# Attention outputs split into 16-bit halves and turned by a crossbar DMA transpose

## What is computed

```python
x = x + 0.5 * _L0_ffn_ref(_layernorm(x, axis=-1), ...)     # ternary weights, 128 -> 512 -> 128
x = x + _L0_attn_ref(_layernorm(x, axis=-1), ...)          # 16 heads of 64, causal, gated outputs
x = x + 0.5 * _L0_ffn_ref(_layernorm(x, axis=-1), ...)
x = x + 0.5 * _L1_ffn_ref(_layernorm(x, axis=-1), ...)     # 8 experts, the best 2 of each token
x = x + _L1_attn_ref(_layernorm(x, axis=-1), ...)          # 16 heads of 64, causal
x = x + 0.5 * _L1_ffn_ref(_layernorm(x, axis=-1), ...)
```

## Time and profile before

| | |
|---|---|
| time, median of 3 runs | 1004.79 us |
| the 3 runs | 1001.63, 1004.79, 1005.98 us |
| span of the profiled execution, first to last instruction | 1000.9 us |
| busy: TensorE / VectorE / GpSimd / ScalarE | 90% / 79% / 73% / 67% of the span |
| TensorE's granted clock, mean | 0.978 of full speed |
| first attention: first to last `project_out` | 72.2 to 362.1 us |
| second attention: the same | 561.6 to 838.2 us |

### The profile page before, as it was taken

One profiled execution on the slowest core, in us unless ns is written; L12 is line 12 of the kernel. 1 busy time (PEld: TensorE's weight loads), 2 busy tenths in 40 slices (PEclk: granted clock), 3 DMA queues, 4 the chain that ended last, 5 costly groups with the idle time before them and its releaser, 6 DMA issues.

```text
span 1000.9 us, 33897 instructions
## 1 busy us (share of the span) xinstructions
PE 897.1 (90%) x13160; PEld 640.5 (64%) x13160; DVE 792.1 (79%) x2394; ACT 673.5 (67%) x1183; POOL 734.7 (73%) x685
## 2 busy tenths in 40 slices
PE   5789999999999879899987899999999985998884
PEld 3467676776777656566654676777677764666663
DVE  6889898888889877777656889888888887866563
ACT  6688888878877626556555787767767762545552
POOL 6789989889887745666545999878888883666662
PEclk9999999999999979999999999999999997999997
DMA  5201011010030001122111000000000001121222
GB/s 153 78 10 45 3 45 45 3 45 2 3 107 3 2 20 39 52 43 85 38 30 51 3 3 3 12 3 2 13 3 3 13 2 30 41 43 44 86 62 82
DMA packets 21118, 33.79 MB, mean 34 GB/s; under 512 B 4578, under 2 KB 10466, under 8 KB 20964
## 3 DMA queue, kind: packets, MB, share of 16 engines
q1 hardware_dynamic: 13728, 18.50, 5.9%
q0 software_dynamic: 5888, 12.07, 4.8%
q10 hardware_dynamic: 1348, 1.05, 0.3%
HBM read 22.44 MB, written 9.18 MB: 32 GB/s over the span
## 4 chain that ended last, share of the span: by engine, by line
PE 63%; DVE 18%; ACT 6%; issue 6%; POOL 3%; another core or an unknown queue 2%; DMA 1%; SPq 0%; POOLq 0%; DVEq 0%; ACTq 0%
PE ps L1698 8%; PE ps L1889 8%; PE ps L1700 8%; PE ps L1699 7%; DVE arena L1308 4%; PE ps L1919 3%; PE ps L2128 3%; PE ps L1853 3%; PE ps L1920 3%; PE ps L1921 3%; PE ps L2140 2%; PE ps L2141 2%; PE ps L2142 2%; PE ps L1864 2%
## 5 line engine op out<-in xcount | busy, mean ns | idle before, releaser
L784 POOL TENSOR_TENSOR arena<-arena 128x1024 f16<-128x1024 f32 x190 | 344.9, 1816 | 86.2 <-ACT arena L980 75.9
L1308 DVE CUSTOM_DVE_ANT_0 arena<-ps,mask_qk 128x512 bf16<-128x512 f32 (+3 forms) x512 | 224.4, 485 | 25.0 <-PE ps L1853 23.8
L972 ACT ACTIVATE arena<-ps,lift 128x1024 f32<-128x1024 f32 (+1 forms) x192 | 186.7, 972 | 85.0 <-PE ps L1899 82.2
L1889 PE MATMUL ps<-arena 64*128 64x512 f16 (+3 forms) x1536 | 148.5, 299 | 10.2 <-ACT arena L972 6.8
L835 POOL DMA_INDIRECT arena<-x_rows,arena x92 | 92.6, 1006 | 88.5 <-PE ps L2103 43.7
L1919 PE MATMUL ps<-arena 128*128 128x65 f16 x1280 | 130.9, 195 | 0.2 <-DVE arena L1332 0.2
L1920 PE MATMUL ps<-arena 128*128 128x64 f16 x1280 | 130.4, 193 | 0.0
L1921 PE MATMUL ps<-arena 128*128 128x65 f16 x1280 | 130.0, 194 | 0.0
L843 POOL DMA_INDIRECT y_rows<-arena x92 | 90.8, 987 | 49.0 <-ACT arena L1138 26.1
L1919 PEld LDWEIGHTS ps<-arena 128*128 128x128 f16 x1280 | 117.4, 98 | 8.4 <-issue 0.5
L1920 PEld LDWEIGHTS ps<-arena 128*128 128x128 f16 x1280 | 117.9, 99 | 0.2 <-issue 0.2
(11 more groups left out here) (288 smaller groups left out, 2695.9 us busy)
## 6 DMA issues: line engine op xcount, KB each, us to landing
stage<-in_L_ffn_W SPq DMA_DIRECT2D x4, 1024.0 KB, 5.3
arena<-y_rows SPq DMA_DIRECT2D x14, 256.0 KB, 3.6
x_rows<-XN SPq DMA_DIRECT2D x8, 256.0 KB, 2.1
arena<-x_rows,arena POOLq DMA_INDIRECT x92
y_rows<-arena POOLq DMA_INDIRECT x92
stage<-in_L_attn_Wkv SPq DMA_DIRECT2D x2, 512.0 KB, 8.3
X<-in_L_attn_tokens SPq DMA_DIRECT2D x3, 256.0 KB, 5.1
out_x<-X SPq DMA_DIRECT2D x3, 256.0 KB
```

The lines of the kernel that those rows point to most:

```text
L784: g.tensor_tensor(PL[:, b, :, cols], P32[:, :, cols], PH[:, b, :, cols], ALU.subtract).then_inc(s_pl, 1)
L972: a_.activation(P32[:, :, UNIT_AT[u]:UNIT_AT[u] + UNIT_W[u]], ps[:, 4:6, 0:UNIT_W[u]], ACT.Exp, bias=lift[:]).then_inc(s_ex_p, 1)
L1308: v_.tensor_tensor_reduce(masked[:, x, 0:w], ps[:, 2 + x, at:at + w], mask_qk[:, CH - w:CH], 1.0, NEG, ALU.add, ALU.max, accum_out=MX[:, i ...
L1889: mm(ps[:, 4 + x, at:at + w], keys, queries, start=(n_ == 0 and part == 0), stop=False)
```

## The change

The outputs are no longer turned as float32 by TensorE. They are split where they stand, with tokens on partitions, and both halves are turned by one DMA through the crossbar, issued by SyncE:

1. ScalarE rounds `O32` to float16 into `OS[:, 0]` (`output_high`), at the place of `turned_high`.
2. VectorE subtracts into `OS[:, 1]` (`output_low`), at the place of `turned_low`.
3. SyncE waits for that and issues one `dma_start_transpose` of `OS` (128 partitions x 1024 float16, 256 KB) into `OT` (128 x 2 x 4 x 128), which lies in the memory of `T32`.
4. TensorE waits for the DMA before `project_out`, which reads `OT`.

TensorE's four transposes per item and their bank are gone, so `outputs(1)` no longer waits for `turned_low`. SyncE's program is rewritten so that its other DMAs stand between the transposes, at given turns. The second normalization writes its intermediate in place into PSUM, since `T32` is taken.

```diff
-        OTh = carve([CH], F16)
-        OTl = carve([CH], F16)
+        OS = carve([2, CH], F16)
+        OT = T32[:].bitcast(F16).rearrange("p (k i d) -> p k i d", k=2, i=TPB)
...
+            def attention(a):
+                base = a * ITEMS
+                def body(t):
+                    o = items(t)[4]
+                    if o is not None:
+                        j = base + o
+                        sp.wait_ge(s_o_lo, j + 1)
+                        if j >= 1:
+                            sp.wait_ge(s_op_ps, j)
+                        sp.dma_start_transpose(OT.rearrange("p k i d -> p (k i) d"), OS.rearrange("p k c -> p (k c)")
+                                               ).then_inc(s_o_turned, 16)
+                    if a == 0 and t == 0:
+                        expert_block(0)
+                    if a == 0 and t == 1:
+                        expert_block(1)
+                    if a == 0 and t in (6, 10, 14, 18):
+                        expert_block((t - 6) // 4 + 2)
+                    if a == 0 and t == 27:
+                        second_layer()
+                    if t in ROWS_OUT[a]:
+                        rows_out(*ROWS_OUT[a][t])
+                run_items(body, range(TURNS))
+            ROWS_OUT = ({20: (3, 0), 28: (3, 1)}, {13: (5, 0), 21: (5, 1), 29: (5, 2)})
...
-                    def turned_high():
+                    def output_high():
                         j = base + o
-                        act.wait_ge(s_ot_ps, j + 1)
-                        if o >= 1:
-                            act.wait_ge(s_op_ps, j)
-                        a_.activation(OTh, ps[:, 7, :], ACT.Copy).then_inc(s_oth_sb, 1)
+                        act.wait_ge(s_o_ev, j + 1)
+                        if j >= 1:
+                            act.wait_ge(s_o_turned, 16 * j)
+                        a_.activation(OS[:, 0], O32.rearrange("p a x d -> p (a x d)"), ACT.Copy).then_inc(s_o_hi, 1)
...
-                    step(v_.tensor_scalar(T32[:], src, gamma[:], beta[:], ALU.mult, ALU.add))
-                    ins_ = v_.tensor_tensor(l, T32[:], h, ALU.subtract)
+                    step(v_.tensor_scalar(src, src, gamma[:], beta[:], ALU.mult, ALU.add))
+                    ins_ = v_.tensor_tensor(l, src, h, ALU.subtract)
...
-                    def turned_low():
-                        dve.wait_ge(s_oth_sb, base + o + 1)
-                        v_.tensor_tensor(OTl, ps[:, 7, :], OTh, ALU.subtract).then_inc(s_otl_sb, 1)
+                    def output_low():
+                        dve.wait_ge(s_o_hi, base + o + 1)
+                        v_.tensor_tensor(OS[:, 1], O32.rearrange("p a x d -> p (a x d)"), OS[:, 0], ALU.subtract
+                                         ).then_inc(s_o_lo, 1)
...
-                        elif v >= 1:
-                            pe.wait_ge(s_otl_sb, j)
...
-                    def turn_outputs():
-                        pe.wait_ge(s_o_ev, base + o + 1)
-                        for i in range(TPB):
-                            ins_ = nc.tensor.transpose(ps[:, 7, i * P:(i + 1) * P],
-                                                       O32[:, i].rearrange("p x d -> p (x d)"), ident[:])
-                        ins_.then_inc(s_ot_ps, 1)
-
                     def project_out():
-                        pe.wait_ge(s_otl_sb, base + o + 1)
+                        pe.wait_ge(s_o_turned, 16 * (base + o + 1))
...
-                            blk = slice(i * P, (i + 1) * P)
-                            split_mm(ps[:, 1, i * D:(i + 1) * D], OTh[:, blk], OTl[:, blk],
+                            split_mm(ps[:, 1, i * D:(i + 1) * D], OT[:, 0, i], OT[:, 1, i],
                                      WOh[:, o % PAIRS], WOl[:, o % PAIRS], s_op_ps if i == TPB - 1 else None)
```

More of the change, by code:

```diff
@@ L342, in macaron_block @@
         s_o_ev = sem("o_ev")
-        s_ot_ps = sem("ot_ps")
-        s_oth_sb = sem("oth_sb")
-        s_otl_sb = sem("otl_sb")
+        s_o_hi = sem("o_hi")
+        s_o_lo = sem("o_lo")
+        s_o_turned = sem("o_turned")
         s_op_ps = sem("op_ps")
@@ L574, in _, with expert_block @@
             sp.dma_start(wg_in[:, HEADS:HEADS + EXPERTS], ins["L1_ffn_Wg"]).then_inc(s_wa_in[4], 16)
-            for i, (src, hi, lo) in enumerate(experts):
+            def expert_block(i):
+                src = experts[i][0]
                 if i == 0:
@@ L587, in _, with second_layer @@
                 sp.dma_start(dst, src).then_inc(s_e_in[i % 2], 16)
[L589 to L592, removed]
+            def second_layer():
+                sp.wait_ge(s_lo_pool, 2 + 4 * len(experts))
+                flat = stage[:].rearrange("p a b -> p (a b)")
+                sp.dma_start(flat[:, 0:3 * INNER].rearrange("p (c d) -> p c d", d=D), wqkv1).then_inc(s_w1_in, 16)
+                sp.dma_start(flat[:, 3 * INNER:4 * INNER], wout1).then_inc(s_w1_in, 16)
@@ new lines, in rows_out, with results_in @@
+            def rows_out(n, c):
+                sp.wait_ge(s_ln_xn, NORM_NO[n, c])
+                at = c % HCH * CH
+                sp.dma_start(x_rows[c // HCH][at:at + CH].rearrange("(p t) d -> p t d", t=TPC),
+                             XN[:, TPC * c:TPC * (c + 1), :]).then_inc(s_x_rows[c // HCH], 16)
+            def results_in(m, h):
+                for k in range(YRING):
+                    sp.wait_ge(s_y_out[k], moved(m, k, HT * (h + 1)))
+                for c in range(HCH * h, HCH * (h + 1)):
+                    for j in range(TOPK):
+                        at = j * TOK + c * CH
+                        sp.dma_start(Yt[:, c, j], y_rows[at:at + CH].rearrange("(p t) d -> p t d", t=TPC)
+                                     ).then_inc(s_y_got[c], 16)
@@ L604, in end_loads @@
                              ).then_inc(s_out_done, 16)
[L606 to L622, removed]
             x_out = out.rearrange("b (t p) d -> p (b t) d", p=P)
@@ L631, in stored @@
                                  ).then_inc(s_out_done, 16)
-            moe(3, 0)
-            moe(5, 1)
+            attention(0)
+            rows_out(3, 2)
+            rows_out(3, 3)
+            results_in(0, 0)
+            results_in(0, 1)
+            attention(1)
+            rows_out(5, 3)
+            results_in(1, 0)
+            stored(0)
             end_loads()
@@ L1033, in body @@
                     if o is not None:
-                        turned_high()
+                        output_high()
                     if s is not None:
@@ L1359, in evacuate @@
                         if v >= 1:
-                            dve.wait_ge(s_ot_ps, j)
+                            dve.wait_ge(s_o_lo, j)
                         v_.tensor_tensor(O32.rearrange("p a x c -> p x a c"), o4[:, :, :, 0:DH],
@@ L1390, in body @@
                     if o is not None:
-                        turned_low()
+                        output_low()
                     if t == TURNS - 3:
@@ L1955, in body @@
                             project_k()
-                    if o is not None:
-                        turn_outputs()
                     if s is not None:
```

## The result

| | before | after |
|---|---|---|
| median | 1005.98 us | 1075.44 us |
| runs | 1001.63 to 1009.18 us (5) | 1072.96 to 1082.27 us (5) |
| profiled execution: time, span | | 1082.27, 1080.5 us |

The ratio is 1.0707, with a 95% interval of 1.0667 to 1.0746. The forecast of 1273 us is far too high. The time lies inside the range, and within a microsecond of the rival called "A short stall, the clock holds" (1076 us). The profiled execution after is the slowest of its five, while the span before (1000.9 us) belongs near the fastest: the two spans differ by 79.6 us, the medians by 69.5 us.

What follows compares the result with a forecast made beforehand. TensorE was taken to bound the attentions. Span 1000.9 + 187 (stall) - 21 (transposes removed) + 102 (clock) = 1269 us, median 1273; range 1050 to 1540 us.

Steps and rivals of the forecast that it cites:

- A short stall, the clock holds: Rival: transfer of 2.4 to 3.6 us in 256 B pieces, no clock fall; 1076 us at 3.5; chance 0.16.
- What bounds the kernel: In the attentions TensorE, busy 90% of a 1000.9 us span, is what a microsecond has to be taken from.
- 2.0 us of cover: Distance from the end of VectorE's low half to `project_out`, into which the DMA goes; 128 us over 63 items.
- D: Transfer time from the end of VectorE's low half to TensorE's release: 5.0 us, chosen between 3.5 and 8.2.
- the stall: TensorE's wait at `project_out` for what the transfer exceeds the cover by: 63 x 5.0 - 128 = 187 us.
- my two piece counts: Crossbar transfer per DMA engine: 64 pieces of 256 B give 3.5 us, 512 of 32 B give 8.2 us.
- My estimate of 10.5 us: Transfer time from the skill's transpose page, eight blocks one after the other; the sum would then be 1616 us.
- The clock: After TensorE waits of some 3.0 us the granted clock falls, losing 1.7 us in 60 turns: 102 us.
- The transposes' worth: Removing TensorE's four transposes, 0.53 us a turn, gains a mean 0.35 us in 60 full turns: -21 us.
- nothing catches up: With `scores(0)` behind `project_out`, all exponentials, maxima and low halves of the next turn wait too.
- SyncE and the halves: 64 transposes added to SyncE's queue, and the halves in their old places and sizes, were costed at nothing.
- The formula without the clock: Span of 1000.9 + 63 times the transfer time - 149 us, leaving out the 102 us for the clock.

Runs made afterwards that it cites:

- x_no_transfer: The changed kernel without its DMA: `project_out` reads the halves unturned, so the product is wrong; 963.93 us, 0.9955 of the kernel before.
- x_early: The changed kernel with `output_high` first in ScalarE's turn and `output_low` ahead of VectorE's `maxima(0)`; 1019.24 us, 1.0518 of the kernel before.
- x_unread: The changed kernel with the DMA still issued, but `project_out` reads the unturned halves without waiting for it; 965.13 us, 0.9964 of the kernel before.
- x_fewer_pe: The changed kernel without one of three products with the values, 20 TensorE matmuls a turn fewer; 1019.54 us, 1.0529 of the kernel before.
- x_twice: The changed kernel with each transpose made twice, the second after the first has landed; 1300.56 us, 1.3409 of the kernel before.
- x_after_again: The changed kernel again without edit, on a faster chip, as base for the runs beside it; 1045.04 us, 1.0792 of the kernel before.

## Why the prediction was wrong

**What bounds the kernel: right.** TensorE's path through a turn, and the 2.0 us of cover, held: 1.9 to 2.0 us also in x_no_transfer.

**D, the wrong step.** "I take 5.0 us between these, nearer to the first": it was 2.8 us undisturbed and 3.5 on average. With 63 x 1.5 = 94 us this is the larger part of the stall's error: forecast 187, measured 88. The lower of my two piece counts was right (64 pieces of 256 B an engine), but even its 3.5 us is 0.7 too long for an undisturbed transpose. I had added 64 pieces at 22 ns to the whole 2.1 us of a plain 256 KB, which already holds the time of its own bytes. The trace has, from the end of the low half, 0.03 us to the issue, 1.18 to the first packet, 1.08 for the packets (18 ns each) and 0.53 from the last one to TensorE's start, 2.82 in all. That disturbed ones take 0.4 to 2 us more I did not foresee; it brings the mean to 3.5.

The Trainium skill's rule that transposing DMAs are as fast as plain ones ("Advanced Engine Details and Errata", section X-Bar Transpose) comes close by this trace: in x_early a transpose lands in 2.8 us and a plain `x_rows<-XN` of as many bytes in 2.3, in x_unread in 3.0 and 3.1. It would still have misled, since by it D was to be 2.1 us and the kernel faster, and the path to TensorE decides at 2.4 us. The Trainium skill's page "VectorE: DVE Perf Modes" (section The three transpose paths) gives 1309 ns for one 128x128 block. My estimate of 10.5 us from it, with eight blocks one after the other, does not hold: eight in one transfer take 2.26 us from issue to last packet. (The sum at 10.5 us is 1615 us, not 1616.) One block alone no run here shows.

**The clock: the price right, the count wrong.** "I charge 1.7 us in 60 turns: 102 us." A turn with a fallen clock is 1.5 or 1.6 us longer (the rest of it 8.45 instead of 6.84 us, or 7.95 instead of 6.49), but there are only some ten such turns, since the waits are mostly shorter. TensorE is at half clock for 96 us in 15 stretches after, and for 47 us in 8 before; half of the difference is 25 us. Also the rule by which I charged them is too simple. Of the 14 waits of 1.8 to 2.8 us for a transpose, eight are followed by 5.2 us at 0.50 to 0.72, and six by 1.00, though they are as long. Windows behind a wait of 2.25 us and one of 2.45 us, columns as in the earlier trace rows:

```profile
628.40:633.60 5.20, 4.97 (x51) 2.75 (x53) 3.54 (x14) 2.01 (x3) 4.97 (x6) 0.72 0.00 0
751.40:756.60 5.20, 4.97 (x69) 2.83 (x70) 3.48 (x9) 3.13 (x4) 2.73 (x3) 1.00 0.00 0
```

It also fell behind shorter waits than I had allowed for, one of 1.49 us here and one of 1.28 us in x_fewer_pe. In x_twice, with a wait of 3 us or more in 62 of 64 items, the clock falls behind 60 of them, and there the term comes near. What decides for a shorter wait stays open.

**The transposes' worth: -21 forecast, -4.4 measured when nothing waits.** The sum over turns was wrong in that it let every turn gain; some 20 us come back as waits for ScalarE and VectorE. In the changed kernel itself the rest of the turns is 10.1 us shorter although the clock costs it some 25, so that some 35 us come off there. Turns that stay at 7.72 us in x_no_transfer take 6.84 to 6.89 us in after in three of four cases. In the turn to item 17 TensorE waits 0.55 us for the exponential in x_no_transfer; in after, behind a wait of 2.38 us for the transpose of item 16, it waits for nothing until the next transpose. So the stall gives VectorE and ScalarE time to be done, and pays some of itself back. I had written that nothing catches up; this was wrong. It is read from these waits (36.8 us in the three rows above, 22.9 us in the same rows of after), not tested by an experiment of its own.

**SyncE and the halves: right.** x_unread shows queue and traffic at no cost that can be told. The low half from SBUF takes 689 ns where it took 686.

**The sum.** The formula without the clock gives 1072 us at the measured mean of 3.5, and the span was 1080.5. That is partly luck: it leaves out 25 us of clock and 14 us of what the stall gave back beyond my 21, and its case has no clock falling. The chance of 0.16 for this case was too small: its bound of D came from the nearest rows, while 5.0 us came from no row.

## What to carry to other kernels

Before a DMA is put on the path of an engine, measure the distance that it has to fit in (here 2.0 us, a row each turn) against the whole handover, from the end of the writer to the start of the reader: with 256 KB or half of that it was mostly fixed time, so splitting it saves little (0.4 us). The price of a plain transfer from the trace holds its bytes already: adding pieces on top counts them twice. Where a DMA's wait is close to its cover, its spread counts as much as its middle, and other queues on the same DMA engines (here the fetching of TensorE's own program) set the spread. To move a step earlier for more cover is a change to the engine that it is moved on: test the order without the transfer first. And work taken off a busy engine is worth its own time only where no other engine is about to hold it (34 us gave 4.4).

## What the runs showed of the hardware

- A crossbar transpose of 128 partitions x 1024 float16: the issuing instruction 1.23 us, first packet at 1.18 us, last at 2.26 us, 1024 packets of 256 B at 18 ns, 257 to 291 GB/s; from the end of VectorE's instruction to TensorE's start 2.82 us.
- When a 16 KB instruction packet (0.9 to 1.6 us) starts between 0.3 and 2.25 us behind its issue, the issue itself is longer (1.7 to 2.5 us), or the data end late (3.2 to 4.2 us), or the data are in time and the last of the 16 completions is late (4.2 to 4.5 us against 2.75). All add 0.4 to 2 us. 30 of 64 were hit, 28 of 64 in x_after_again, and with 12% fewer TensorE instructions a turn 12 of 64. That the packet is the cause is shown by this change of the count; how it holds up the others is not. Three slow transposes have another cause, which stays open.
- The granted clock does not fall after every wait of the same length: 1.00 behind one of 2.73 us, 0.72 behind one of 2.25 us, and it fell behind one of 1.49 us.
